# The eight normalisations of the x tiles in a batch, on GpSimd instead of VectorE

## The reference

```python
def _gn(v, G=32, eps=1e-5):
    g = v.reshape(B_, G, C_ // G, H_, W_)
    return ((g - mean(g)) / jnp.sqrt(var(g) + eps)).reshape(v.shape)

q, k, v = (jnp.einsum('btc,hcd->bhtd', xs, W) for W in (Wq, Wk, Wv))
scores = jnp.einsum('bhtd,bhsd->bhts', q, k) * scale
out = jnp.einsum('bhts,bhsd->bhtd', softmax(scores), v)
x = x + (out.transpose(0, 2, 1, 3).reshape(B, T, -1) @ Wproj + bproj)
```

## Time and profile before

| what | value |
|---|---|
| median of 3 runs | 4494.25 us (4492.64 to 4494.88) |
| the profiled execution's own time | 4494.51 us |
| its span | 4492.0 us |
| TensorE busy | 4432.9 us, 99% |
| weight loads busy | 3611.0 us, 80% |
| ScalarE busy | 2999.5 us, 67% |
| GpSimd busy | 2860.8 us, 64% |
| DVE busy | 2644.2 us, 59% |
| TensorE's granted clock | 0.999 of full speed |

### The profile page before, as it was taken

How to read it: one execution, slowest core, us unless ns; L and a number is a source line. 1 busy time by engine, 2 the same in 40 slices (tenths; PEclk the granted TensorE clock), 3 DMA queues, 4 the chain that set the end, 5 groups by cost and what they waited for, 6 DMA issues and landing times.

```text
span 4492.0 us, 61781 instructions
## 1 busy us (share of the span) xinstructions
PE 4432.9 (99%) x20864; PEld 3611.0 (80%) x20864; DVE 2644.2 (59%) x5031; ACT 2999.5 (67%) x5640; POOL 2860.8 (64%) x2223
## 2 busy tenths in 40 slices
PE   8999999999999999999999999999999999999999
PEld 6878788887887878888888888877888878887887
DVE  6665646656466565655656566565664656646554
ACT  5766757667576675766757667575675756757576
POOL 4666666666666666665666656666566666666567
PEclk9999999999999999999999999999999999999999
DMA  2111111111111111121111111111112111111101
GB/s 76 39 43 57 35 57 38 48 52 36 56 38 53 49 37 59 34 59 42 37 58 39 59 42 33 60 40 60 40 32 60 45 59 35 35 61 43 59 23 57
DMA packets 156825, 211.42 MB, mean 47 GB/s; under 512 B 56544, under 2 KB 57568, under 8 KB 156512
## 3 DMA queue, kind: packets, MB, share of 16 engines
q1 hardware_dynamic: 156512, 207.47, 16.0%
HBM read 105.12 MB, written 34.08 MB: 31 GB/s over the span
## 4 chain that ended last, share of the span: by engine, by line
PE 90%; DVE 5%; ACT 2%; issue 1%; DMA 1%; POOL 1%; SPq 0%; ACTq 0%; POOLq 0%; DVEq 0%
PE bank L654 15%; PE bank L706 10%; PE bank L866 10%; PE bank L700 9%; PE bank L868 9%; PE bank L867 9%; PE bank L699 9%; PE bank L666 8%; PE bank L684 8%; DVE xs L1048 1%; DMA xs<-in_x 1%; DVE smax L1081 1%; PE bank L672 1%; ACT prob_h L884 1%; DVE spread L1039 1%
## 5 line engine op out<-in xcount | busy, mean ns | idle before, releaser
L1257 POOL TENSOR_TENSOR prob_l<-prob,prob_h 128x512 fp32r<-128x512 f32 x1660 | 2142.7, 1295 | 1443.5 <-ACT prob_h L884 1406.0
L1081 DVE TENSOR_REDUCE smax<-bank 128x1 f32<-128x512 f32 x2048 | 1345.6, 683 | 843.9 <-PE bank L706 833.9
L884 ACT ACTIVATE prob<-bank 128x512 f32<-128x512 f32 x2048 | 1231.2, 601 | 685.9 <-PE bank L700 601.1
L884 ACT ACTIVATE prob_h<-bank 128x512 fp32r<-128x512 f32 x2048 | 1230.7, 601 | 401.6 <-PE bank L868 308.7
L699 PE MATMUL bank<-q_hh,k_hl 128*128 128x512 f32 x2048 | 830.4, 405 | 0.2 <-DMA q_lm<-q_lm 0.2
L866 PE MATMUL bank<-prob_h,vh 128*128 128x512 f32 x2048 | 816.5, 399 | 5.8 <-ACT acc L994 4.2
L700 PE MATMUL bank<-q_lm,k_h 65*128 65x512 f32 x2048 | 811.8, 396 | 0.0
L867 PE MATMUL bank<-prob_h,vl 128*128 128x512 f32 x2048 | 807.0, 394 | 0.0
L868 PE MATMUL bank<-prob_l,vh 128*128 128x512 f32 x2048 | 806.3, 394 | 0.0
L706 PE MATMUL bank<-k_hl,q_hh 128*128 128x512 f32 x2048 | 709.2, 396 | 4.1 <-DVE smax L1081 3.7
L1019 DVE TENSOR_TENSOR prob_l<-prob,prob_h 128x512 fp32r<-128x512 f32 x388 | 315.0, 812 | 299.5 <-ACT prob_h L884 299.4
(11 more groups left out here) (76 smaller groups left out, 5080.9 us busy)
## 6 DMA issues: line engine op xcount, KB each, us to landing
xs<-in_x SPq DMA_DIRECT2D x252, 256.0 KB, 2.9
q_hh<-q_hh SPq DMA_DIRECT2D x256, 128.0 KB, 2.2
k_hl<-k_h SPq DMA_DIRECT2D x256, 128.0 KB, 2.3
inv_b<-inv_dram SPq DMA_DIRECT2D x256, 128.0 KB, 2.8
out_x<-xs SPq DMA_DIRECT2D x128, 256.0 KB, 2.0
q_lm<-q_lm SPq DMA_DIRECT2D x256, 2.0 KB
den<-acc SPq DMA_DIRECT2D x256, 2.0 KB, 1.7
inv_dram<-inv SPq DMA_DIRECT2D x256, 2.0 KB, 1.4
```

Source lines behind the costliest of these rows:

```text
L884: return nc.scalar.activation(out, ps[ST + bank][:, :], ACT.Exp, scale=SCALE)
L1081: nc.vector.tensor_reduce(smax[:, 2 * t + half:2 * t + half + 1], ps[SM + turn][:, :], AX.X, ALU.max).then_inc(rows_used, 1)
L1257: nc.gpsimd.tensor_tensor(prob_l[:, r3, :], prob[:, ring2, :], prob_h[:, r3, :].bitcast(F32), ALU.subtract).then_inc(prob_l_pool, 1)
```

## The change

The function `norm` of the step loop moves from DVE's queue to GpSimd's, with the same slots. Within a slot it stands behind the low part, `normalise` and `rsqrt`. The prologue keeps its normalisations on DVE. `normalise` at slot 13 of heads 3 and 6 gets a wait on `xn_ready`, for the normalisations that stand before it in the same queue. GpSimd's line numbers in the changed file differ by a few: L1252 is the low part, L1280 the multiplication by the inverse sum, L1234 the root, L1287 the normalisation.

```diff
--- before.py
+++ after.py
@@ -1193,11 +1193,6 @@
                         reciprocal(s, -1, 1)
                     if i == INV_SLOTS[0]:
                         reciprocal(s, 0, 0)
-                    if s.h in (3, 6) and s.has_next:
-                        half = int(s.h == 6)
-                        for t in range(4):
-                            if NORM_SLOTS[half][t] == i:
-                                norm(t, xs[:, t, :], s.batches(2, 2 + half + 1))
 
             def reciprocal(s, ahead, tc):
                 if not (s.section == "first" and tc == 0):
@@ -1278,10 +1273,19 @@
                     blocks = min(s.out_slots[tc] + 1 + AHEAD, BLOCKS if end else 99)
                     done = sum(j % BLOCKS in pool_blocks_of(s, j // BLOCKS) for j in range(blocks))
                     pool.wait_ge(prob_l_pool, s.heads(per_pool, 0, done))
+                if s.h in (3, 6) and s.has_next and tc == 0:
+                    half = int(s.h == 6)
+                    pool.wait_ge(xn_ready, s.batches(8, 8 + 4 * half + sum(at < s.out_slots[0] for at in NORM_SLOTS[half])))
                 pool.wait_ge(inv_in, s.heads(32, ahead, 16 * (tc + 1)))
                 nc.gpsimd.tensor_tensor(o[r, h // 2, tc * 512:(tc + 1) * 512], acc[r, tc, :], inv_b[r, :],
                                         ALU.mult).then_inc(o_ready, 1)
                 pool.wait_ge(o_ready, s.heads(2, ahead, tc + 1))
+
+            def norm(t, count):
+
+                pool.wait_ge(rstd_ready, count)
+                nc.gpsimd.tensor_scalar(xs[:, t, :], xs[:, t, :], gmean[:, t:t + 1], rstd[:, t:t + 1],
+                                        ALU.subtract, ALU.mult).then_inc(xn_ready, 1)
 
             def split_out(s, t):
 
@@ -1309,6 +1313,11 @@
                     if any(kind == "var" for kind, a in s.takes[i]):
                         entry_taken(pool, s, "var", 0 if s.h == 3 else 1)
                         rsqrt()
+                    if s.h in (3, 6) and s.has_next:
+                        half = int(s.h == 6)
+                        for t in range(4):
+                            if NORM_SLOTS[half][t] == i:
+                                norm(t, s.batches(2, 2 + half + 1))
                     if s.proj and i in SPLIT_SLOTS:
                         split_out(s, SPLIT_SLOTS.index(i))
                     if s.proj and i in PROJ_SLOTS:
```

## The result

The changed kernel takes 4583.69 us, median of 4 runs, against 4493.44 for the kernel before; the ratio is 1.0199 (95% interval 1.0181 to 1.0217). It is 90 us slower. I had forecast 4506, slower by 12, in a range up to 4526. The direction was right, the size was wrong by a factor of seven, and the time is outside the range.

A forecast was written before the change was run, and what follows sets the result against it. TensorE, busy 99%, was taken as the bound: block 1's matmul 1.08 us late less 0.31 kept at tile 6 gave net +0.8 us a batch, times 15 +12 us on 4494.25, so 4506 us; range 4488 to 4526.

The forecast's parts named there:

- the bound from above on d: Length d of one normalisation on GpSimd: at most 1.30 us, a two-input op's length; 0.87 us was taken.
- Block 1's end: End of the low part of head 7's key block 1 on GpSimd: forecast 273.8, its matmul 1.08 us later than before.
- the DVE term: Seam of heads 6 and 7: two DVE low parts push GpSimd's queue back 0.6 us each, 1.20 us a batch.
- without such a lock: If DVE and GpSimd did not hold each other for whole instructions, the lateness would be 1.2 us a batch less.
- It waits at a tile's transpose longer than now: Sign of being wrong: TensorE waiting longer at a tile's transpose; the forecast had the wait for the normalised tile gone.
- Head 3: Two normalisations ahead of L1282 and two behind the next low part fit GpSimd's idle gaps: cost 0.
- The gain side: TensorE's three late steps at the seam of heads 6 and 7: at most 0.90 us a batch, 13.5 us in fifteen.
- Rival 2: A normalisation on GpSimd costs as much as any two-input op, 1.30 us: 4525 us; chance 0.18, with d above 1.05.
- Rival 3: DVE's relief arrives in full at the seam: -0.90 us a batch, -13.5 us, 4481 us; chance 0.07.
- Rival 4: GpSimd doesn't let DVE in while it has work queued: +1.5 to +3 us a batch, 4517 to 4540; chance 0.06.

The follow-up runs named there:

- 256 columns: The changed kernel with GpSimd normalising only columns 0 to 255 of each tile, the others left as they are: 4502.4 us, ratio 1.0022 to the kernel before.
- 8 columns: The changed kernel with GpSimd normalising 8 of 512 columns, queue order and waits kept: 4476.82 us, ratio 0.9967 to the kernel before.
- tile 6 behind block 1: The changed kernel with tile 6's normalisation one slot later, behind the low part of block 1 of head 7: 4568.84 us, ratio 1.0168 to the kernel before.

## Why the prediction was wrong

**The step that failed is the bound from above on d.** I took "two-input, 1.30 us" as the upper end for a one-input instruction, because it reads one tensor less. The measured length is 2.08, outside my bounds, and every time in the forecast is a function of it. The rows from which I worked (a memset, an affine_select, tensor_tensor) are each another instruction; that they lay between 0.53 and 1.30 said nothing of a fourth. The estimate by the GPSIMD Engine Reference of the Trainium skill (section 3.1: 1.03 cycles an element with at most two operations) was 0.67; the measured 3.34 ns is 4.0 cycles of 1.2 GHz. The measurement decides: that rate does not hold for this instruction.

**The sum, with the right length.** Block 1's end was 269.99 + 3d, and 1.2 for two DVE low parts. With 2.07 it is 277.4, and the matmul 4.7 us late. Measured in the first batch is 277.56, less the 0.87 us that the seam had already shifted: 3.9 late. The difference is the DVE term: the low part of block 0 did not push GpSimd back at all, and that of block 2 by 0.3. I had taken two pushes of 0.6 us from the reading that a low part of DVE and an op of GpSimd hold each other for their whole length, which does not hold for this instruction (see the last section); my sentence "without such a lock" had 1.2 us less, measured are 0.9. In time: with d = 2.07 the sum gives 4.37 us a batch, 66 us; less 0.9 a batch, 52; the two heads of the seam lost 8.0 + 63.6 = 72, of which the clock has 21, so 51. At 256 columns, where one takes 1.22 us, the sum gives 28 and not 24, and the same term takes 14 off; measured are 9, and the last 5 us I did not trace (8 columns gave 4 us more than counted as well).

The order of the queue and the waits that I named for block 1 (L866 for prob_l, ScalarE's exp behind it) were right. That no other would come was wrong, and follows from d as well: with the first normalisation at 268.23 + 2.07 = 270.30, tile 4 itself is late, and TensorE waits 0.92 us for it in each batch where it was to wait no more and had waited 0.26. "It waits at a tile's transpose longer than now" was my own sign of being wrong, and it came; head 6, in which it stands, loses 8.0 us.

**Head 3** was put at nothing because of a bound of 1.3 us a normalisation; past that, block 3 was to slip by the excess. It slipped by 2.5 us, of which TensorE felt 0.93, 14 us in all. The pair behind block 1's low part takes 4.58 us in a gap of 2.61, an excess of 2.0; the other 0.6 comes from the pair ahead of L1280, 4.15 us and two short waits in a gap of 3.76, which I had called longer and not summed.

**The gain side** was close: 13.5 us counted, 17 measured with 8 columns.

**The clock** was not in the forecast. It takes 21 to 23 us of the 84, more than the forecast as a whole. It has the opposite sign of the error in the DVE term and nearly its size (14), so a sum with the right d alone would have come near the measured loss at the seam (66 against 72) by luck. A stall of 3.1 us is neither enough (none in three of the 15 batches) nor needed: with tile 6 behind block 1, where two stalls of 1.1 and 1.2 us start 2.2 us apart, the clock fell in 10 batches (0.996). In the profiled executions whose stalls at the seam stayed single and under 1.3 us it was 0.999 or 1.0. What exactly brings it down I did not test.

**The rivals.** Rival 2 (as slow as a two-input instruction) had the direction and still fell short. Rival 3 (DVE's relief in full) is what a free normalisation would give, and does give with 8 columns. Rival 4 (GpSimd keeps DVE out) is refuted: DVE's low part is let in even while a normalisation runs, see below.

## What to carry over

An instruction whose length no row shows has to be measured before its cost is bounded: a neighbouring form on the same engine is no upper bound, even if it reads more. Where work moves to an engine whose idle time is scattered, sum what its queue holds between two deadlines, at the seam with the least room, since the busy share (64% here) says nothing of it. A stall can also cost more than its length: here the clock that fell behind it took a quarter of the loss. And a look at who holds a slow instruction can be worth more than moving it: one L1282 a slot later gave 7 us, the move cost 90.

## What the runs showed of the hardware

GpSimd's tensor_scalar on 128 x 512 float32 takes 2.08 us with two operations and 1.50 with one, more than its tensor_tensor (1.295).

It does not hold DVE for its whole length, as a tensor_tensor does. Three low parts of DVE in the changed kernel, which take 0.69 us alone:

```profile
181.71 1.01 DVE L1019 TENSOR_TENSOR prob_l<-prob,prob_h 128x512 fp32r<-128x512 f32 x1 [0.73 <-ACT prob_h L884]
...
269.02 0.69 DVE L1019 TENSOR_TENSOR prob_l<-prob,prob_h 128x512 fp32r<-128x512 f32 x1 [0.93 <-ACT prob_h L884]
...
273.41 0.93 DVE L1019 TENSOR_TENSOR prob_l<-prob,prob_h 128x512 fp32r<-128x512 f32 x1 [2.30 <-ACT prob_h L884]
```

The first starts 0.31 us into a normalisation (181.40) and takes 1.01, so it was held for 0.32, until 0.63 us into it. The second starts 0.79 us into one (268.23) and is not held, nor is that one lengthened. The 30 low parts in this trace that start later than 0.55 us into a normalisation (they all start at 0.77 or more) take 0.69 each. The 34 that start 0.6 to 1.0 us into an L1280 take 0.88 to 1.23. The third, at 273.41, runs into the end of L1280, and the normalisation that follows at 273.89 takes 2.39. So it seems to be done with what it shares with DVE after some 0.6 us; what it does for the other 1.4 no run shows. The page SBUF — State Buffer of the Trainium skill (SBUF: two separate sides) says that the shared pair of ports is held for the whole instruction; for GpSimd's tensor_scalar these rows say otherwise.
